# Attention opened by halves of the tokens, with GpSimd's share of the opening moved to VectorE

## What is computed

```python
x = x + 0.5 * F(layernorm(x))      # opening f = 0
x = x + R(layernorm(x))            # "rwkv"
x = x + 0.5 * F(layernorm(x))      # opening f = 1
# F(t) = h + moe(rmsnorm(h, norm2_w)),  h = t + attention(rmsnorm(t, norm1_w))
# attention: 16 query heads, 4 key/value heads of 128; q, k = rope(t@wq), rope(t@wk); v = t@wv
#   rope([x1, x2]) = [x1*cos - x2*sin, x2*cos + x1*sin];  causal softmax(q.k/sqrt(128)) @ v @ wo
# R ends in  x2 + sigmoid(xc@Wcr) * (relu(xcs@Wck)**2 @ Wcv)
```

## Time and profile before

| | |
|---|---|
| median of 3 runs | 1224.39 us (1222.77 to 1224.81) |
| the profiled execution | 1219.8 us, of which the span is 1217.9 us |
| busy, share of the span | PE 96%, DVE 77%, ACT 66%, POOL 50% |
| first projection to first turning, f = 0 | 18.04 to 42.62 us |
| the same, f = 1 | 673.01 to 696.31 us |
| last `value` matmuls of rwkv end | at 663.3 us |

### The profile page before, as it was taken

One profiled execution on the slowest core, in us unless ns is written; L12 is line 12 of the kernel. 1 busy time (PEld: TensorE's weight loads), 2 busy tenths in 40 slices (PEclk: granted clock), 3 DMA queues, 4 the chain that ended last, 5 costly groups with the idle time before them and its releaser, 6 DMA issues.

```text
span 1217.9 us, 19172 instructions
## 1 busy us (share of the span) xinstructions
PE 1165.5 (96%) x6690; PEld 982.5 (81%) x6690; DVE 936.5 (77%) x2010; ACT 797.9 (66%) x1561; POOL 604.9 (50%) x449
## 2 busy tenths in 40 slices
PE   5899999999999899999998899999999999989998
PEld 4788888888888668887687688888888888848887
DVE  6777887787788686767887777787788788677775
ACT  5666666676666467776565766666666666557774
POOL 4666666666671234440001394775765763224452
PEclk9999999999999999999999999999999999999999
DMA  5100100100022753452101100010010011663334
GB/s 184 40 1 1 40 1 1 40 1 1 1 66 65 231 154 59 86 122 61 57 1 37 38 1 1 8 32 1 1 40 1 1 41 30 216 190 71 52 51 98
DMA packets 50671, 64.64 MB, mean 53 GB/s; under 512 B 5920, under 2 KB 37792, under 8 KB 50400
## 3 DMA queue, kind: packets, MB, share of 16 engines
q1 hardware_dynamic: 37904, 47.68, 11.8%
q0 software_dynamic: 10560, 13.64, 7.3%
q10 hardware_dynamic: 2112, 2.10, 0.5%
HBM read 51.60 MB, written 13.11 MB: 53 GB/s over the span
## 4 chain that ended last, share of the span: by engine, by line
PE 86%; DVE 5%; ACT 4%; DMA 2%; issue 2%; POOL 1%; SPq 0%; DVEq 0%; ACTq 0%; POOLq 0%
PE ps L1715 22%; PE ps L1717 21%; PE ps L1716 21%; PE ps L1785 10%; PE ps L1882 6%; PE ps L1866 1%; DMA sum_dram<-ys,row_of 1%; PE ps L1696 1%; ACT probs L856 1%; PE ps L1837 1%; PE ps L1970 1%; PE ps L1940 1%; ACT probs L883 1%; PE ps L1814 1%; DVE h L1271 0%
## 5 line engine op out<-in xcount | busy, mean ns | idle before, releaser
L856 ACT ACTIVATE probs<-ps,negmax 128x128 f32<-128x128 f32 (+7 forms) x256 | 189.6, 741 | 88.8 <-DVE negmax L1249 84.9
L862 ACT ACTIVATE probsT<-ps 128x512 fp32r<-128x512 f32 x288 | 170.2, 597 | 112.0 <-PE ps L1785 110.6
L1255 DVE TENSOR_TENSOR probsT<-ps,probsT 128x512 fp32r<-128x512 f32 x288 | 196.0, 685 | 46.2 <-ACT probsT L862 44.2
L1249 DVE CUSTOM_DVE_ANT_0 ps<-ps,causal 128x128 f32<-128x128 f32 (+7 forms) x256 | 193.4, 761 | 28.7 <-PE ps L1717 26.2
L710 POOL TENSOR_TENSOR crossed<-crossed,rope 128x512 f32<-128x512 f32 x70 | 90.4, 1292 | 191.2 <-ACT crossed L842 191.1
L1785 PE MATMUL ps<-square,probs 128*128 128x128 f32 x1152 | 170.3, 273 | 5.7 <-ACT probs L856 5.3
L1785 PEld LDWEIGHTS ps<-square,probs 128*128 128x128 f32 x1152 | 140.6, 140 | 35.0 <-issue 4.2
L1372 DVE TENSOR_TENSOR parts<-experts,parts 128x1024 fp32r<-128x1024 f32 x92 | 112.2, 1225 | 56.4 <-ACT parts L906 56.4
L1271 DVE SCALAR_TENSOR_TENSOR h<-ps,rowinv,h 128x256 f32<-128x256 f32 x256 | 123.4, 483 | 35.4 <-PE ps L1717 27.0
L1715 PE MATMUL ps<-keysT,queriesT 128*128 128x512 f32 (+4 forms) x384 | 142.0, 370 | 3.2 <-DVE straight L1225 1.4
L1716 PE MATMUL ps<-keysT,queriesT 128*128 128x512 f32 (+4 forms) x384 | 131.1, 341 | 0.0
(11 more groups left out here) (275 smaller groups left out, 2859.6 us busy)
## 6 DMA issues: line engine op xcount, KB each, us to landing
experts<-in_L_ffn_w_dram SPq DMA_DIRECT2D x48, 512.0 KB, 7.4
w_in<-in_L_ffn_wq_dram SPq DMA_DIRECT2D x8, 512.0 KB, 3.9
wo_in<-in_L_ffn_wo_dram SPq DMA_DIRECT2D x8, 512.0 KB, 6.1
rows_dram<-probs ACTq DMA_DIRECT2D x4, 512.0 KB, 3.6
probs<-in_L_attn_x_dram SPq DMA_DIRECT2D x2, 512.0 KB, 4.8
w_in<-in_L_ffn_wk_dram SPq DMA_DIRECT2D x8, 128.0 KB, 4.7
straight<-in_L_ffn_wv_dram SPq DMA_DIRECT2D x2, 512.0 KB, 6.1
rope<-in_c_rope_dram SPq DMA_DIRECT2D x1, 1024.0 KB, 4.9
```

Source lines behind the costliest of these rows:

```text
L856: act.activation(probs[:, i % 2, k, 0:w], ps[:, 2 * slot_n:2 * slot_n + 2, :].rearrange("p b n -> p (b n)")[:, at:at + w], ACT.Exp, bias=n ...
L862: act.activation(probsT[:, m % 3, 0, :], ps[:, 4 + m % 2, :], ACT.Copy).then_inc(S["probsT_high"], 1)
L1249: dve.tensor_tensor_reduce(out=row, in0=row, in1=causal[:, T - w:T], scale=-1.0, scalar=LARGEST, op0=ALU.add, op1=ALU.min, accum_out=negma ...
L1255: dve.tensor_tensor(probsT[:, m % 3, 1, :], ps[:, 4 + m % 2, :], probsT[:, m % 3, 0, :].bitcast(F32), ALU.subtract).then_inc(S["probsT_low ...
```

## The change

- **By halves.** The norms, `h`, `y`, the transposes and `tokT` are made for tiles 0 to 3 first. The first projections need this half alone. The other half is done by steps put into `FIRST`: `late_sqrt`, `late_scales`, `late_y`, `late_turn`, `late_high`, `late_low`, `late_h`. `y` is now made from x with a scale and a bias, not from `h`, so it needn't wait for `h`. At f = 0 VectorE makes `y` of three tiles (`Y_DVE`).
- **At f = 1** the first half's norms, `h`, `y`, transposes and `tokT` are put in among `value(4)` to `value(7)` and `gated_value(4)` to `(7)`; x is stored in two halves.
- **GpSimd's steps** in `FIRST` (the sines and two low parts), the value weights' low part and, at f = 1, the low part of the query and key weights go to VectorE. GpSimd keeps the low part of the query weights at f = 0, and it now splits `w_o[0]` at both f, after `qk_low` of all five blocks and after all of `h`.
- **Order.** `qk_sum`, `qk_high` and `qk_low` come one block earlier in the lists, and so does `v`; the late transposes and `v` of tile 2 stand between the projections and the scores. The Exp table is loaded by a small activation between the first two `crossed`.
- **Loads at f = 0.** The second half of x comes after the weights; norm1_w and the first halves of the cosines and sines come before the value weights. Token ids and the gate's scaling on VectorE move behind `SECOND`.
- **TensorE** runs 20 spare matmuls at the start and 8 after the first four tiles' transposes.

```diff
+OPENING_SPINS = (20, 8)
+Y_DVE = 3
...
-        if n >= 2:
-            pe += [("v", n - 2, 0)]
+        pe += [("v", n - 1, 0)] if n in (1, 2) else []
+    pe += [("late_turn", t, 0) for t in range(NT // 2, NT)]
+    pe += [("v", 2, 0)]
...
-        act += [("qk_high", *_first[n - 2])] if 0 <= n - 2 < blocks else []
+        act += [("late_sqrt", 0, 0)] if n == 0 else []
+        act += [("qk_high", *_first[n - 1])] if 0 <= n - 1 < blocks else []
+        act += [("late_y", t, 0) for t in (2 * n, 2 * n + 1)] if n in (2, 3) else []
+        act += [("late_high", c, 0) for c in range(DC)] if n == 4 else []
...
-        dve += [("straight", *_first[n])] if n < blocks else []
-        dve += [("qk_sum", *_first[n - 1])] if 0 <= n - 1 < blocks else []
-        dve += [("qk_low", *_first[n - 2])] if 0 <= n - 2 < blocks and not on_pool(n - 2) else []
+        dve += [("straight", *_first[n]), ("times_sines", *_first[n])] if n < blocks else []
+        dve += [("late_scales", 0, 0)] if n == 0 else []
+        dve += [("qk_sum", *_first[n])] if n < blocks else []
+        dve += [("qk_low", *_first[n - 1])] if 0 <= n - 1 < blocks else []
+        dve += [("late_low", c, 0) for c in range(DC)] if n == 4 else []
+        dve += [("late_h", NT // 2, 0)] if n == 4 else []
...
-        pool += [("times_sines", *_first[n])] if n < blocks else []
-        pool += [("qk_low", *_first[n - 2])] if 0 <= n - 2 < blocks and on_pool(n - 2) else []
+        dve += [("late_h", t, 0) for t in range(NT // 2 + 1, NT)] if n == early - 2 else []
...
+                            sp.dma_start(cols[:, :, N1], column("L0_ffn_norm1_w")).then_inc(S["n1_in"], 16)
+                        sp.dma_start(x[:, 4:NT, :], x_dram[:, 4:NT, :]).then_inc(S["x_in_last"], 16)
+                        rope_dram = a["c_rope"].rearrange("p (k t) -> p k t", k=2)
+                        sp.dma_start(rope[:, :, 0:HALF], rope_dram[:, :, 0:HALF]).then_inc(S["rope_in"], 16)
...
-                    sp.wait_ge(S["x_final"], 1)
-                    sp.dma_start(sum_tiles[1], x).then_inc(S["saved"], 16)
+                    sp.wait_ge(S["cv_used"], NT // 2)
+                    sp.dma_start(sum_tiles[1][:, 0:4, :], x[:, 0:4, :]).then_inc(S["saved"], 16)
+                    sp.wait_ge(S["cv_used"], NT)
+                    sp.dma_start(sum_tiles[1][:, 4:NT, :], x[:, 4:NT, :]).then_inc(S["saved_late"], 16)
...
-                if f == 0:
-                    pool.wait_ge(S["consts_in"], 16 * 3)
-                group(f, 0, FIRST)
-                if f == 0:
-                    pool.wait_ge(S["qk_ready"], len(_first))
-                    pool.wait_ge(S["consts_ready"], 1)
-                    split(f * KVH, w_o[0], wo_in[:], "wo_in", 16, "wo_split")
+                    pool.wait_ge(S["h_ready"], NT // 2)
+                    first_weights()
+                    pool.wait_ge(S["rope_in"], 16)
+                    pool.wait_ge(S["rope_late"], 16)
+                pool.wait_ge(S["qk_ready"], 10 * KVH * f + len(_first))
+                pool.wait_ge(S["h_ready"], NT * (f + 1))
+                pool.wait_ge(S["consts_ready"], 1)
+                split(f * KVH, w_o[0], wo_in[:], "wo_in", 16, "wo_split")
...
+                    if what == "late_sqrt":
+                        stream_sqrt(1)
+                        act.activation(half[:, 1:2], half[:, 0:1], ACT.Exp)
...
+            def take_y(f, t):
+                act.wait_ge(S["scales_ready"], 2 * f + t // 4 + 1)
+                act.activation(y[:, t, :], x[:, t, :], ACT.Identity, scale=std[:, 0, t:t + 1], bias=std[:, 1, t:t + 1]
+                               ).then_inc(S["y_ready"], 1)
+            def token_high(f, half, c):
+                act.wait_ge(S["n1_in"], 16)
+                act.wait_ge(S["turned"], NT * f + 4 * half + 4)
+                act.activation(tokT[:, 0, c, half * HALF:(half + 1) * HALF], ps[:, 2 * c + half, :], ACT.Copy,
+                               scale=cols[:, c, N1:N1 + 1]).then_inc(S["tokT_high"], 1)
+            def stream_start(f):
+                for t in range(0 if f else Y_DVE, NT // 2):
+                    take_y(f, t)
+                if f == 0:
+                    first_weights(f)
+                for c in range(DC):
+                    token_high(f, 0, c)
+                value_weights(f)
...
-                act.wait_ge(S["wo_in"], 16 * (KVH + 1))
-                act.activation(w_o[0][:, 0], wo_in[:], ACT.Copy).then_inc(S["wo_split"], 1)
+                stream_sqrt(0)
+                stream_start(1)
...
+            def scales(half, n):
+                cols4 = slice(4 * half, 4 * half + 4)
+                dve.wait_ge(S["std_ready"], n)
+                link(dve.reciprocal(rstd[:, :, cols4], std[:, :, cols4]))
+                link(dve.tensor_tensor(std[:, 0, cols4], rstd[:, 0, cols4], rstd[:, 1, cols4], ALU.mult))
+                dve.scalar_tensor_tensor(out=std[:, 1, cols4], in0=meanvar[:, cols4, 0], scalar=-1.0, in1=std[:, 0, cols4],
+                                         op0=ALU.mult, op1=ALU.mult).then_inc(S["scales_ready"], 1)
+            def take_h(t):
+                dve.tensor_scalar(h[:, t, :], x[:, t, :], meanvar[:, t, 0:1], rstd[:, 0, t:t + 1],
+                                  ALU.subtract, ALU.mult).then_inc(S["h_ready"], 1)
...
+                    scales(0, stream_norms(0))
+                    for t in range(Y_DVE):
+                        dve.tensor_scalar(y[:, t, :], x[:, t, :], meanvar[:, t, 0:1], std[:, 0, t:t + 1],
+                                          ALU.subtract, ALU.mult).then_inc(S["y_dve"], 1)
+                    dve.wait_ge(S["first_key"], 1)
+                    dve.tensor_tensor(w_qkv[:, 1, :, REP * HD:], w_in[:, :, REP * HD:], w_qkv[:, 0, :, REP * HD:].bitcast(F32),
+                                      ALU.subtract).then_inc(S["first_key"], 1)
+                    for t in range(NT // 2):
+                        take_h(t)
+                    for c in range(DC):
+                        token_low(f, 0, c)
+                    dve.wait_ge(S["x_in_last"], 16)
+                    for t in range(NT // 2, NT):
+                        last = dve.bn_stats(stats[:, t, :], x[:, t, :])
+                    link(last)
+                    value_weights(f)
+                    late[0] = stream_norms(1)
...
+                    if what == "times_sines":
+                        n, (_, across) = grp.qk_n((i, k)), grp.terms((i, k))
+                        dve.tensor_tensor(across, across, rope[:, 1, 0:HALF], ALU.mult).then_inc(S["sines_in"], 1)
...
-                for n in range(4, NT):
-                    last = gated_value(n)
-                link(last)
-                dve.sem_inc(S["x_final"], 1)
+                first_half = stream_norms(0)
+                dve.wait_ge(S["w_split"], 2 * KVH + 1)
+                dve.tensor_tensor(w_qkv[:, 1], w_in[:], w_qkv[:, 0].bitcast(F32), ALU.subtract).then_inc(S["w_split"], 1)
+                scales(0, first_half)
+                gated_value(4)
+                for t in range(NT // 2):
+                    take_h(t)
+                gated_value(5)
+                for c in range(DC):
+                    token_low(1, 0, c)
+                value_weights(1)
+                gated_value(6)
+                link(gated_value(7))
+                late[0] = stream_norms(1)
...
+                if f == 0:
+                    pe.wait_ge(S["dve_step"], 1)
+                    spin(OPENING_SPINS[0])
+                    pe.wait_ge(S["square_in"], 16)
+                    for t in range(NT // 2):
+                        turn_tokens(f, t)
+                    spin(OPENING_SPINS[1])
+                pe.wait_ge(S["xT_ready"], NT * f + 4)
...
-                for n in range(4, NT):
-                    value(n)
+                value(4)
+                value(5)
+                pe.wait_ge(S["cr_sig"], NT)
+                for t in range(NT // 2):
+                    turn_tokens(1, t)
+                value(6)
+                value(7)
...
```

More of the change, by code:

```diff
@@ L1134, in _ @@
             rwkv()
-            sqrt(2)
             attention(1)
@@ L1236, in group @@
                         dve.wait_ge(S["qk_high"], len(_first) * f + grp.qk[i, k] + 1)
-                        dve.wait_ge(S["qk_ready"], n)
                         dve.tensor_tensor(dst[:, 1], direct, dst[:, 0].bitcast(F32), ALU.subtract
                                           ).then_inc(S["qk_ready"], 1)
+                    if what == "late_scales":
+                        scales(1, late[0])
+                    if what == "late_h":
+                        take_h(i)
+                    if what == "late_low":
+                        token_low(f, 1, i)
                     if what == "v_low":
```

188 lines of the change are left out of this document (90 added, 98 removed).

## The result

The changed kernel takes **1213.94 us** (median of 5 runs, 1213.71 to 1215.19), and the kernel before, run beside it, 1222.77 (1220.71 to 1224.81). The ratio is 0.9928 [0.9910, 0.9945]: faster by 0.7%, and faster than the 1219.0 us of the forecast. The profiled execution of the changed kernel took 1213.9 us, of which the span is 1212.1; that of before took 1219.8, with 1217.9.

A forecast was written before the change was run, and what follows sets the result against it. TensorE was taken as the bound. Earlier projections (9.0 + 5.1) less longer openings (3.1, 2.6) and 1.2, 0.5, 0.3, 1.0 gave 5.4 us: 1214.4 against the profiled 1219.8, plus 4.6 to the median, 1219.0; range 1214.0 to 1224.0.

The forecast's parts named there:

- What bounds it: Whole kernel: TensorE, busy 96% of the span; other engines matter only where it stands, as between rwkv and first projection.
- P at f = 1: Start of the second opening's first projection, interleaved with rwkv's last value steps: 664.0, which is 9.0 us earlier.
- P at f = 0: Start of the first opening's first projection, at the kernel's start: 12.9, which is 5.1 us earlier.
- D: Each opening, first projection to first turning: 27.2 us at f = 0, 26.4 at f = 1; 2.6 and 3.1 longer.
- Behind the turning: After each opening's first turning: losses of 1.2 us for `late_h`, 0.5 for GpSimd's split, 0.3 for the gate's scaling.
- The split's 0.5: GpSimd splitting `w_o[0]` behind the last `late_h` delays its rotation of `kk` 3.3 us at f = 1; 0.5 us lost.
- The clock: TensorE's granted clock more likely to fall at the f = 1 opening: 1.0 us lost, bounds 0 and 1.8.
- Rival 4: Both openings: idling holds TensorE at 1.2 GHz before the turning, 2.5 to 3 us more each; 1225.6 us, chance 0.08.
- The table rule: ScalarE's Exp table load in the openings: skill states 1.28 us load plus 1.38 drain; forecast took the load alone.
- Rival 2: Behind the turning, GpSimd's split makes row 4's scores wait for q1 blocks, about 3 us more: 1222, chance 0.12.
- Rival 3: TensorE stands before `value(6)` in rwkv, waiting for late `y`; 3 us lost: 1222, chance 0.05.
- Rival 1: Slack absorbs `late_h`, GpSimd's lateness and the clock: 1216.0 us, or 1214.2 with the f = 0 fall spared; chance 0.25.

The follow-up runs named there:

- the repeat: Kernel before and changed kernel measured and profiled once more, nothing edited: before 1223.33 us (12 runs); changed 1214.69 us (9 runs), ratio 0.9943 against before beside it.

## Why the prediction was right and wrong

**What bounds it** held. GpSimd has left the chain, and TensorE's gap behind rwkv, closed by the interleaving, is most of the gain. Undoing that alone loses all of it.

**P at f = 1**: the middle is shorter by 9.00 us. The root was ready in time: table load at 650.89, norms applied from 654.20, transposes at 654.99, with TensorE busy throughout. The query weights' low part took 1.48 us at 650.09 and the value weights' 1.22 at 658.36, both in the places named for them. The 0.75 that I had for `late_h` and the gate behind the first turning don't show in it. **P at f = 0**: 12.76 against 12.9.

**D**: 27.46 and 26.93 against 27.2 and 26.4. VectorE's list was the right ground: from the first `straight` (664.42) to the first `max` (679.40) VectorE stands once, for 0.62 us behind the table load. Sums and sines took 0.69 and 0.68, for 1.287 before. The walk gave the first `max` at 17.65, measured is 17.79; from there to the turning it is 9.1 us where I had 8.8. The prediction charged VectorE 3.05 us for the five sines and gave back 3.0 for the faster sums, so their move came out at nothing, and my later expectation put 0 to 1 us on the other side. Up to the first `max` it is worth 2.9 and 1.6 us, because GpSimd slows not only the sum but other VectorE instructions that run beside it, and VectorE waits for it besides. The mistake was to think that leaving the work with GpSimd relieves VectorE by its full length.

**Behind the turning**: rest without a fall that costs is 522.1 to 522.3 against 521.6, so 0.5 to 0.7 us for `late_h`, the gate and the split together, where I had 1.25. The split's 0.5 was a wrong part: GpSimd's rotation of `kk` starts at 695.04, 6.5 us behind the turning, 2.9 later than before where I had 3.3, and taking the lateness away gained nothing.

**The clock**: a second fall at f = 1, as thought likely. Its price was 1.2 to 1.4 us, mine 1.0. Rival 4 (a fall inside the opening) isn't in the changed kernel's first profile, but it is in others: with the early table left out, and, at 32 to 36 and 681 to 684, in the changed kernel's second one, where D was 27.80 and 27.22: 0.3 us longer each, not 2.5.

**The table rule** (Trainium skill, ScalarE: Activation LUTs, What ACT_TABLE_LOAD costs) did not show in its drain, only in the load itself: the load at 664.71 takes 1.28, the next activation starts 0.01 us behind its end, and block 1's `crossed` stands at P + 4.61, for which the row gave 4.7.

**The other rivals.** Rival 2 needs waits of TensorE for GpSimd. The waits of the changed kernel's TensorE from 640 to 800 us (in total, times, longest) have none:

```profile
PE ps L1869 <- ACT probs L857: 2.7, 2, 2.0
PE ps L1791 <- ACT probs L857: 2.7, 2, 2.4
PE ps L1791 <- DVE probs L1276: 0.8, 1, 0.8
PE ps L1771 <- ACT probs L896: 0.7, 1, 0.7
PE ps L1791 <- DVE straight L1276: 0.7, 1, 0.7
```

Rival 3 would show as a gap between 650 and 664, and there is none. Rival 1 was nearest, with 1216.0, and for part of its reason: `late_h` and GpSimd's lateness cost little, but the clock did cost. That its second figure, 1214.2, is almost the median is luck: it supposes that the fall at f = 0 is spared, and the fall stands at 41 us in the profile.

**The step that failed** is the last of the sum: "The median of the runs, 1224.39, lies 4.6 us above that execution; taking it over gives 1219.0". Against the profiled execution I had 1214.4, and the changed kernel's was 1213.9. Its median, 1213.94, lies on its own profiled execution, and the forecast was 5.1 us too high: 0.5 from the sum of the parts, 4.6 from this step. The 4.6 us were no constant of the program. Some 1.3 of them were the median of three runs, 1224.39 where 84 executions have 1223.1. The other 3.3 were the place of one execution among its like: the profile of before had caught one at a clock of 0.997, the median goes with about 0.991, and in the repeat the profiled execution lies 0.6 above its median. The changed kernel has 0.0 the first time and 1.75 in the repeat, where its median of 1214.69 would have been 4.3 us under the forecast. The sum prices an undisturbed execution; the range should have taken the 4.6 us as an unknown with bounds 0 and 4.6, and so reached some 4 us lower.

**What stays open** is why the changed kernel loses so little of this. The share of clock that it loses is about the same in the mean of its repeat (0.991 over 9 runs, 0.992 over 12 of before), and the time that goes with it is half. A part can be read from the profiles: it matters where the falls stand. The changed kernel's second profiled execution has five of them (32, 418, 428, 681 and 1066 us) and yet spans 1211.1, 1.0 less than the first, which has only the two at the turnings (each has one more in its last microseconds). The two inside its openings, where VectorE sets the pace, cost 0.3 us each, the one at 1066 nothing, and at the turnings there is none. Whether this makes the whole difference is not shown, since one execution or two of each kernel were profiled. The low clock in the gap behind rwkv isn't the reason, nor a cold start, nor a fall at the turnings: spare matmuls in each left the median of before where it was. Waits for gathered tokens at full clock, as in two profiled executions above, are a second source; how often they come isn't known. That GpSimd's work in the openings plays a part is not shown either; sines back on GpSimd gave a spread of 3.3 us over 12 runs, less than before's. The falls of the executions that took over 1225 us weren't seen one by one.

## What to carry to other kernels

Before a sum is carried from a profiled execution to a median, look at the granted clock of both: where one program's executions scatter by 0.7%, the distance between the two isn't a term that stays. Where two executions of one program differ, follow the same instruction in both: a stretch at a low clock may have cost nothing, and the time may be lost elsewhere. The work that stood between rwkv and the projection cost TensorE nothing once each of its steps had a place among the last products of rwkv, and walking through each queue found P and D to about half a microsecond. GpSimd's elementwise work beside VectorE was a cost of both engines here.

## What the runs showed of the hardware

- One program: 84 executions from 1217.96 to 1227.44 us, going with the mean granted clock (correlation -0.93). Falls of 3 to 10 us stood at other places in each profiled execution, often behind 1 to 2.5 us of idling (the end of attention at 415 and 1060, the turnings). A short one (3 to 4 us) cost nothing at 1066, 0.3 inside the changed kernel's openings, 1.2 to 1.4 at its second turning and 1.7 at 592.
- At a granted clock of 1.00, GpSimd's issue of a gather took 2.02 us in place of 1.01 in one execution, and TensorE fell behind by 2.3 us.
- Spare matmuls in an idle time took the fall away from there, and it came elsewhere (32 to 37, 414 to 425, 1060 to 1072); over 42 runs of five kernels with more of them than their own base no median went down by what can be measured.
- VectorE's 128x512 low part took 0.69 us alone and 1.77 beside GpSimd's multiplication of 1.28, and the sum before took 1.287. A 128x4 step took 1.07 beside GpSimd's multiplication from 15.62 to 16.91 us (the kernel with the sines on GpSimd) and 0.16 with GpSimd idle (the changed kernel, f = 1):

```profile
15.87 1.07 DVE L1193 TENSOR_TENSOR var<-meanvar,std 128x4 f32<-128x4 f32 x1
```

```profile
649.82 0.16 DVE L1187 TENSOR_TENSOR var<-meanvar,std 128x4 f32<-128x4 f32 x1
```
